# Moving the slot table, two early loads of x, W0's sum and its lo part to other engines, and the last slot's first y sums to other PSUM banks

## What is computed

```python
def _L0_cond_ref(x, weights, condition):        # weights (16, 64, 64)
    W = weights[condition]
    return jnp.einsum('bct,bcd->bdt', x, W)

def _L1_cond_ref(x, weight, adapter_ids):       # weight (8, 1024, 1024)
    w = weight[adapter_ids]
    return jnp.einsum('bsi,boi->bso', x, w)

x = x + _L0_cond_ref(x, L0_cond_weights, itok_B_0_15)
x = x + _L1_cond_ref(x, L1_cond_weight, itok_B_3_7)
```

## Time and profile before

| | |
|---|---|
| median of 3 runs | 802.09 us (801.84 to 802.85) |
| the profiled execution's own time | 801.83 us |
| its span | 800.1 us |
| PE busy | 780.0 us, 97% of the span |
| DVE busy | 593.5 us, 74% |
| ACT busy | 455.8 us, 57% |
| POOL busy | 249.7 us, 31% |
| chain that ended last | PE 92%, DVE 3%, DMA 1%, SP's queue 1% |

### The profile page before, as it was taken

One profiled execution on the slowest core, in us unless ns is written; L12 is line 12 of the kernel. 1 busy time (PEld: TensorE's weight loads), 2 busy tenths in 40 slices (PEclk: granted clock), 3 DMA queues, 4 the chain that ended last, 5 costly groups with the idle time before them and its releaser, 6 DMA issues.

```text
span 800.1 us, 19241 instructions
## 1 busy us (share of the span) xinstructions
PE 780.0 (97%) x3448; PEld 644.1 (80%) x3449; DVE 593.5 (74%) x708; ACT 455.8 (57%) x772; POOL 249.7 (31%) x156
## 2 busy tenths in 40 slices
PE   4999999999999999999999999999999999999996
PEld 4778888888888888888888888888888888888884
DVE  6868897788887567888876788887566756766665
ACT  2545666566566555665755566566554654555554
POOL 2144444243542212345431243452122122122210
PEclk9999999999999999999999999999999999999998
DMA  7244444344523324444333434532332233233223
GB/s 262 62 126 133 134 143 137 120 121 146 152 92 95 105 80 134 122 149 135 101 104 105 132 114 138 154 101 82 105 105 79 65 105 102 61 99 105 73 85 80
DMA packets 73955, 90.89 MB, mean 114 GB/s; under 512 B 13781, under 2 KB 64470, under 8 KB 73942
## 3 DMA queue, kind: packets, MB, share of 16 engines
q1 hardware_dynamic: 63490, 57.97, 23.4%
q10 hardware_dynamic: 10452, 32.78, 14.6%
HBM read 57.15 MB, written 33.55 MB: 113 GB/s over the span
## 4 chain that ended last, share of the span: by engine, by line
PE 92%; DVE 3%; issue 1%; DMA 1%; SPq 1%; ACT 0%; ACTq 0%; POOL 0%; DVEq 0%; POOLq 0%
PE first_ps L522 14%; PE first_ps L523 14%; PE z_ps L522 14%; PE z_ps L523 14%; PE z_ps L525 14%; PE first_ps L525 13%; PE y_ps L535 7%; DMA w_nat<-in_L_cond_weight_dram 1%; DVE w_lo L735 1%; SPq L428 0%; DVE y L909 0%; SPq L445 0%; DVE z_parts L902 0%; DVE x_turned L894 0%; PE first_ps L503 0%
## 5 line engine op out<-in xcount | busy, mean ns | idle before, releaser
L347 POOL TENSOR_TENSOR xt_lo<-x_turned,xt_hi 128x1024 fp32r<-128x1024 f32 x61 | 146.7, 2406 | 262.4 <-ACT xt_hi L632 259.9
L522 PE MATMUL z_ps<-w_hi,xt_hi 128*128 (+1 forms) x528 | 205.9, 390 | 0.4 <-issue 0.3
L522 PE MATMUL first_ps<-w_hi,xt_hi 128*128 x528 | 205.6, 389 | 0.3 <-POOL xt_lo L347 0.3
L523 PE MATMUL z_ps<-w_lo,xt_hi 128*128 (+1 forms) x528 | 205.4, 389 | 0.0
L523 PE MATMUL first_ps<-w_lo,xt_hi 128*128 x528 | 205.4, 389 | 0.0
L909 DVE TENSOR_TENSOR y<-y_ps,y 64x512 f32<-64x512 f32 x256 | 176.0, 689 | 32.8 <-ACT y L648 26.7
L525 PE MATMUL z_ps<-w_hi,xt_lo 128*128 (+1 forms) x512 | 199.2, 389 | 0.0
L525 PE MATMUL first_ps<-w_hi,xt_lo 128*128 x480 | 186.7, 389 | 0.0
L648 ACT ACTIVATE y<-y_ps 64x512 f32<-64x512 f32 x256 | 151.5, 593 | 12.2 <-issue 2.4
L637 ACT ACTIVATE z_parts<-first_ps 64x512 fp32r<-64x512 f32 x132 | 78.4, 594 | 130.2 <-PE y_ps L535 101.5
L637 ACT ACTIVATE z_parts<-z_ps 64x512 fp32r<-64x512 f32 x132 | 78.4, 594 | 126.9 <-PE y_ps L535 91.1
(11 more groups left out here) (130 smaller groups left out, 354.2 us busy)
## 6 DMA issues: line engine op xcount, KB each, us to landing
x_in<-in_x_dram SPq DMA_DIRECT2D x536, 64.0 KB, 2.5
out_dram<-y ACTq DMA_DIRECT2D x124, 256.0 KB, 3.6
w_nat<-in_L_cond_weight_dram SPq DMA_DIRECT2D x128, 128.0 KB
w_nat<-in_L_cond_weight_dram SPq DMA_DIRECT2D x4, 512.0 KB, 5.5
w_turned<-in_L_cond_weight_dram SPq DMA_DIRECT2D x2, 512.0 KB, 5.6
y<-in_L_cond_weight_dram SPq DMA_DIRECT2D x2, 512.0 KB, 7.0
x_turned<-in_L_cond_weights_dram SPq DMA_DIRECT2D x2, 256.0 KB, 4.1
x_in<-in_x_dram SPq DMA_DIRECT2D x2, 256.0 KB, 4.0
```

Of the source, the lines that this page charges most:

```text
L347: nc.gpsimd.tensor_tensor(xt_lo[h][:], x_turned[h][:], xt_hi[h][:].bitcast(F32), ALU.subtract).then_inc(xt_lo_made, 1)
L522: nc.tensor.matmul(to, xt_hi[h][:, t, :], whi, start=(t == 0), stop=False)
L523: mm = nc.tensor.matmul(to, xt_hi[h][:, t, :], wlo, start=False, stop=last and not pair)
```

## The change

- **Table and early x (SP, ACT).** The DMA that moves the table is issued by SP, behind the eight chunks of the first group, and no more by ScalarE. SP then loads x of slot 1 and x of slot 2 with the sample numbers read from the rows of `table_i` itself, without waiting for the moved table (for slot 2 it waits until x of slot 0 has been transposed, whose place it takes). Only then does it wait for `table_moved` and load the chunks of slots 0 and 1.
- **W0 (POOL, DVE).** W0 is loaded into `w_turned[0]`; chunk 2 of the first group takes `x_turned[1]` instead. GpSimd adds the identity to W0 and makes its lo part, behind its last sum for the first group. VectorE does neither, and waits for W0's lo part after the transpose of x of slot 1.
- **Last slot (PE, ACT, DVE).** The y sums of half 0 go to `z_ps[0]` and `z_ps[1]`, without a wait for `y_made`; half 1 stays in `y_ps[1]`.

```diff
-        w0_nat = x_turned[1][:].rearrange("p t c -> p (t c)").rearrange("p (n d) -> p n d", d=C)
+        w0_nat = w_turned[:, 0].rearrange("p (n d) -> p n d", d=C)
+        first_nat = [w_nat[:, 0], w_nat[:, 1], x_turned[1][:].rearrange("p t c -> p (t c)"), w_turned[:, 1], y[0][:], y[1][:], w_nat[:, 0], w_nat[:, 1]]
...
+        last_y_banks = [z_banks[0], y_ps[1]]
...
+            pool.wait_ge(w0_loaded, 2 * 16)
+            nc.gpsimd.tensor_tensor(w0_nat, w0_nat,
+                                    two_ident[:].rearrange("p (n d) -> p n d", n=1).to_broadcast([P, NCOND, C]),
+                                    ALU.add).then_inc(w0_with_1, 1)
+            pool.wait_ge(w0_hi_made, 1)
+            nc.gpsimd.tensor_tensor(w0_all[:, :, 1], w0_nat, w0_all[:, :, 0].bitcast(F32),
+                                    ALU.subtract).then_inc(w0_lo_made, 1)
...
-            sp.wait_ge(table_moved, 16)
+            sp.wait_ge(table_made, 1)
+            sp.dma_start(slot_row[:, 1:LOOKED_UP + 1, :], table_i[0:LOOKED_UP]).then_inc(table_moved, 16)
...
+            def load_early_x(s, h):
+
+                _, samples = nc.values_load_multi_w_load_instructions(
+                    table_i[s:s + 1, SAMPLE_A:SAMPLE_B + 1], engines=[sp.engine], min_val=0, max_val=B - 1,
...
+            load_early_x(1, 1)
+            sp.sem_inc(x_loaded[0], PER_X)
+
+            sp.wait_ge(first_turned, NH * TURN_OF[X0] + NH)
+            load_early_x(2, 0)
+
+            sp.wait_ge(table_moved, 16)
             pairs_past = look_pairs_past(sp)
-            load_x(1, 1)
...
             load_chunks(0)
-            slot(0, 0)
+            load_chunks(1)
...
             def last_half(pair):
 
                 sum_z(1, 1, buf, pair, range(0, KT // 2))
-                pe.wait_ge(y_made, PER_Y * (2 * pairs_past) + (2 + MADE_AHEAD))
-                sum_y(s, pair, (0,))
+                sum_y(s, pair, last_y_banks, (0,))
...
-            keep_first_hi(0)
-            act.wait_ge(table_made, 1)
-            act.dma_start(slot_row[:, 1:LOOKED_UP + 1, :], table_i[0:LOOKED_UP]).then_inc(table_moved, 16)
-            for i in range(1, len(TURN_ORDER)):
+            for i in range(len(TURN_ORDER)):
                 keep_first_hi(i)
...
-            dve.wait_ge(w0_loaded, 2 * 16)
-            nc.vector.tensor_tensor(w0_nat, w0_nat,
...
-            dve.wait_ge(w0_hi_made, 1)
-            nc.vector.tensor_tensor(w0_all[:, :, 1], w0_nat, w0_all[:, :, 0].bitcast(F32), ALU.subtract).then_inc(w0_lo_made, 1)
...
+            turn_x(0, 1)
+
             dve.wait_ge(w0_lo_made, 1)
-            turn_x(0, 1)
```

More of the change, by code:

```diff
@@ L416, in _, with load_x, load_samples @@
                 load_first(c)
-            sp.wait_ge(table_moved, 16)
-            def load_x(s, h, turned=None):
-                samples = look(sp, s, SAMPLE_A, SAMPLE_B)
-                if turned is not None:
-                    sp.wait_ge(x_is_turned, turned)
+            sp.wait_ge(table_made, 1)
+            sp.dma_start(slot_row[:, 1:LOOKED_UP + 1, :], table_i[0:LOOKED_UP]).then_inc(table_moved, 16)
+            def load_x(s, h):
+                load_samples(look(sp, s, SAMPLE_A, SAMPLE_B), h)
+            def load_early_x(s, h):
+                _, samples = nc.values_load_multi_w_load_instructions(
+                    table_i[s:s + 1, SAMPLE_A:SAMPLE_B + 1], engines=[sp.engine], min_val=0, max_val=B - 1,
+                    skip_runtime_bounds_check_because="the table is made on the chip, of clipped indices")
+                load_samples(samples, h)
+            def load_samples(samples, h):
                 for half, sample in enumerate(samples):
@@ L464, in _ @@
             sp.wait_ge(first_turned, NH * len(TURN_ORDER))
-            sp.sem_inc(x_loaded[0], PER_X)
             load_chunks(0)
-            slot(0, 0)
+            load_chunks(1)
             slot(0, 1)
@@ L527, in sum_z, with sum_y @@
                     mm.then_inc(z_summed, 1)
-            def sum_y(s, pair, halves=range(NH)):
+            def sum_y(s, pair, banks=y_ps, halves=range(NH)):
                 for n in halves:
@@ L908, in add @@
                     own = y[h][rows_of(k), n * HALF:(n + 1) * HALF]
-                    nc.vector.tensor_tensor(own, y_ps[n][k][rows_of(k)], own, ALU.add).then_inc(y_made, 1 if pair else 2)
+                    nc.vector.tensor_tensor(own, banks[n][k][rows_of(k)], own, ALU.add).then_inc(y_made, 1 if pair else 2)
             def finish_y(s, h):
@@ L940, in _ @@
             keep_x0_lo(TURN_OF[X0])
-            for i in range(TURN_OF[X0] + 1, len(TURN_ORDER) - 1):
+            for i in range(TURN_OF[X0] + 1, len(TURN_ORDER)):
                 keep_first_lo(i)
-            dve.wait_ge(w0_loaded, 2 * 16)
-            nc.vector.tensor_tensor(w0_nat, w0_nat,
-                                    two_ident[:].rearrange("p (n d) -> p n d", n=1).to_broadcast([P, NCOND, C]),
-                                    ALU.add).then_inc(w0_with_1, 1)
-            keep_first_lo(len(TURN_ORDER) - 1)
             dve.wait_ge(table_moved, 16)
```

22 lines of the change are left out of this document (11 added, 11 removed).

## The result

| | before | after |
|---|---|---|
| median | 802.37 us (801.84 to 802.85) | 796.61 us (796.19 to 797.35) |
| profiled execution, its span | 801.83, 800.1 us | 796.80, 795.1 us |

The ratio is 0.993, 95% interval 0.9917 to 0.9943: faster by 5.8 us. The forecast was 797.1 (795.9 to 799.4), and its sum, made against the profiled execution, was 796.86 where 796.80 was measured. The traced executions differ by 5.0 us and the medians by 5.8: the one of before lay 0.5 us under its median, the one of after 0.2 above.

The account below looks back on a forecast made before the run. TensorE, busy throughout its middle stretch, was taken as the bound, so only front and end could move. 1.10 + 2.50 + 1.37 = 4.97 us off 801.83 gave 796.86, forecast as a median of 797.1 (795.9 to 799.4).

Parts of the forecast that it names:

- z starts earlier: TensorE's first z matmul at 23.83 us in place of 24.93: 1.10 us gained, bounds 0 and 1.95.
- stalls of the front: TensorE's stalls between 24.93 and 56.56 us, at slot boundaries and for z's lo part, all go: 2.50 us.
- the end: Last slot's y sums skip the wait for VectorE: 1.57 us less 0.20 given back, 1.37 us gained.
- The turns: Transposes before z: VectorE's lo parts begin 1.95 us earlier; GpSimd's unmoved chunk sums then limit the last two turns.
- The boundary of slots 0 and 1: TensorE's stall at 36.36 us for xt_lo goes; W0 on GpSimd costs nothing, with 0.55 or some 2.8 us of cover.
- the tie: VectorE's table step at 25.36 us against GpSimd's W0 lo part at 25.35; if held, it ends at about 27.8.
- Either way the stall goes: Held or not, xt_lo of slot 1 is ready before TensorE wants it at 34.82 us; 0.55 us ahead if held.
- The chunk of group 1: Issued about 29.9 us, on GpSimd at 38.4, TensorE ready at 49.25, wanted at 52.05: stalls at 55.20 and 56.02 go.
- A: VectorE held by W0's work on GpSimd for one further 2.40 us, xt_lo 1.85 late: about 799.0 us; chance 0.11.
- B: Part of the front gain stays away: turns no earlier, 798.2 us, or chunk no earlier, 798.7; chance 0.10.
- C: Slower: the table lands late behind six chunks in SP's queue, 804.8 us if at 36 us; chance 0.04.
- D: The end gives nothing, since the chain through VectorE's add sets it: 798.5 us; chance 0.05.

Follow-up runs that it names:

- e1: c0_bounded with the table's DMA back in ScalarE's queue, x of slots 1 and 2 still loaded early by SP: 801.11 us, 0.9977 of before.
- e3: c0_bounded with W0's sum and lo part back on VectorE: 799.67 us, 0.9958 of before.
- f2_late_x: c1_masked with x of slots 1 and 2 loaded in the late order of before: 800.58 us, 0.9975 of before.
- e2_late_x: c0_bounded with x of slot 1 loaded only after the table has moved, x of slot 2 after it is ready: 804.0 us, 1.0015 of before.
- f5_forced_hold: c1_masked with VectorE waiting for W0's hi part and making two tiny memsets before the table's field: 798.49 us, 0.9944 of before.
- f1_table_on_act: c1_masked with the table's DMA back in ScalarE's queue: 798.16 us, 0.9942 of before.
- f9_two_more_pool: c1_masked with two further unused 128x1024 sums on GpSimd behind W0's lo part: 799.43 us, 0.9957 of before.
- c0_bounded: The changed kernel with chunk and group numbers from the table compared with their limits where they are read: 799.0 us, 0.9951 of before.
- f4: c1_masked with the old end, the last slot's first y sums back in the y banks: 798.65 us, 0.995 of before.
- f10: The kernel before, masked as in c1_masked, with the last slot's change of banks alone: 801.84 us, 0.9988 of before.
- c1_masked: The changed kernel with chunk and group numbers cut to their low bits by one register operation: 798.12 us, 0.9947 of before.

## Why the prediction was right, and where it was lucky

| term of the sum | forecast | measured | by itself, in the experiments |
|---|---|---|---|
| z starts earlier | 1.10 | 1.21 | 0.80 and 1.73 (table), minus 0.35 to 1.08 (early x) |
| stalls of the front | 2.50 | 2.39 | 3.11 and 3.92 (early x), 0.48 and 0.56 (table), 0.07 less to 0.50 (W0) |
| the end | 1.37 | 1.40 | 1.36 and 1.38 |
| sum | 4.97 | 5.00 | |

The last column doesn't add up, since each part uses cover that another one gives. Its values for z's start are differences of two single traces; by groups of traces they are 1.1 (table) and minus 0.8 (early x). In e1 and e3 (0.56 and 0.50) the time is lost behind the front, from 70 us on. That the sum meets the traced execution to 0.06 us is luck on top of that: executions of either kernel scatter by 1 us.

**The turns.** Right: with the table on SP the hi part of turn 1 is made at 13.46 and VectorE's lo parts begin at 15.50 (forecast 15.55). Right too that GpSimd's sum for chunk 6 is late next: it ended at 21.17 (forecast 21.08), and turn 7 began at 21.22 (21.12). From there two errors cancel. The prediction took 2.42 + 0.29 us for the last two turns from the earlier trace rows. In f2_late_x, where both chunks are there, they take 1.81 us (21.19 to 23.00). In the changed kernel they take 2.50, since chunk 7's sum "doesn't move" was wrong: it came 0.91 us later. The step that failed is the one that took chunk 7's row from the trace of before as untouched, although 64 KB transfers were moved to just behind it in the same queue. Where they are late, GpSimd waits 0.19 us for chunk 7 at the most; where they are early, it always did, for 0.92 to 1.47 us. Without that, z would start some 0.7 us earlier yet.

**The boundary of slots 0 and 1.** The stall went, and W0 on GpSimd cost nothing: its two operations lasted 2.40 and 2.41 us as forecast. But the tie that the prediction was afraid of was decided by the same late chunk. The field on VectorE came at 25.28 (forecast 25.36), GpSimd's lo part only at 26.16 (25.35), because W0's sum stood behind chunk 7's. So nothing was held. In e2_late_x and f2_late_x, where chunk 7 is in time, the tie came as forecast (field 25.05, lo part 25.12 and 25.11): the field slipped through, the copy behind it was held and ended at 27.67. "Either way the stall goes" was wrong for the other way: the prediction gave it a cover of 0.55 us, and in f5_forced_hold and f1_table_on_act, where it was held, 0.74 and 0.48 us of Z were lost. The chain from the transpose to TensorE was right (6.02 forecast, 6.11 and 6.12 in the two), but with x early GpSimd's lo part ends at 28.2 to 29.8 and not at 27.8, again because of chunk 7 (with x late it ends at 27.59). The cover without a hold, forecast at 2.8 us, is 2.5 by f9_two_more_pool. The section on who interferes with whom in the Trainium skill, "SBUF — State Buffer", gave the hold rightly: the field, with two inputs in SBUF, waits until GpSimd ends where it starts second (1.47 us in e1, 2.23 in f1), and isn't held where it starts 0.03 us ahead (f5). The prediction took only the field for exposed; the copy behind it, with one input, was held too (2.31 us in e2, f2 and f5).

**The chunk of group 1.** The stalls went, with less to spare than I said. It was issued at 31.10 (forecast 29.9), since the looks between x and the chunk took 3.4 us and not 2, and it reached GpSimd 9.4 us later, not 8.5. VectorE's lo part of slot 1 ends at 49.80 + 1.41 = 51.21, which is 0.75 us before the y matmuls begin; the prediction had 2.8 us there. Counted to the fourth of them, the one that reads it, the cover is 1.3 us; c0_bounded shows how little it takes.

**The end.** Forecast 1.57 less 0.20, measured 1.40. VectorE's add begins at 786.91 and its lo part at 788.35, directly behind, as forecast; ScalarE makes nothing late: its hi part at 787.58 waits 0.49 us for TensorE.

**The rivals.** A (VectorE held for another 2.4 us) did not come; f1 and f5 show its mechanism at a smaller price, since the hold lasts only until GpSimd ends. B has a true part: the early loads do take something from the start. C did not come: the table landed before VectorE asked, whose row at 25.28 shows no idle time. D falls by f4 and f10.

**Left open.** Loading x only once chunk 7 has landed might give back the 0.7 us at the start, but uses up cover of the chunk of group 1, which is 1.3 us; it wasn't run. Why c1_masked's runs scatter by 3 us where the changed kernel's scatter by 1.2, and lie 1 to 1.5 us above them by the median and only 0.5 by the traced span, isn't settled.

## What to carry to other kernels

When transfers are moved to an earlier place in a queue, look at what is still in flight there: the row of the transfer ahead of them is not a constant, even if it was issued first. For each stall that is to go, write down its new cover in us along with the gain; here two covers of 1.3 and 2.5 us carry 2.4 us of gain, and a few register steps at each look-up undid all of it (Z 759.98 in c0_bounded, 759.41 before the change). Count a cover to the very instruction that reads the late part. And two operations of VectorE and GpSimd on SBUF that fall within a microsecond of each other are to be costed at the bad order, whichever one the trace happens to show.
